# Three engines' hand-written step orders in a four-layer cross-attention kernel, placed anew

## What is computed

```python
# layer 0, per batch: channels are the 64 rows, "tokens" the 256 columns
Mn = Wn @ inorm(x) + bn ; Mm = Wm @ inorm(ctx) + bm
A  = softmax(Mn.T @ Mm)                 # 256 x 256
x  = Wo @ ((Wl @ ctx + bl) @ A.T) + bo + x
# layers 1 and 2: 16 heads of 16 features
a  = layer_norm(ctx) * gamma + beta     # over 256 features
Q, K, V = x @ Wq.T, a @ Wk.T, a @ Wv.T
x  = x + tanh(gate) * (softmax(Q K.T / 4, keys masked) V) @ Wo.T
# layer 3: one head of 256
x  = x + alpha * (softmax((x @ wq.T)(ctx @ wk.T).T / 16) (ctx @ wv.T)) @ wo.T
```

## Time and profile before

| | us |
|---|---|
| shown runs, median of 3 (lowest, highest) | 657.51 (656.33, 657.82) |
| profiled execution, its own time | 654.93 |
| its span | 653.1 |
| a round in its middle | 75.2 |
| busy: PE, DVE, ACT, POOL | 579.3, 470.0, 472.2, 118.0 |
| mean granted TensorE clock | 0.972 |

### The profile page before, as it was taken

How to read it: one execution, slowest core, us unless ns; L and a number is a source line. 1 busy time by engine, 2 the same in 40 slices (tenths; PEclk the granted TensorE clock), 3 DMA queues, 4 the chain that set the end, 5 groups by cost and what they waited for, 6 DMA issues and landing times.

```text
span 653.1 us, 25792 instructions
## 1 busy us (share of the span) xinstructions
PE 579.3 (89%) x10867; PEld 507.6 (78%) x10867; DVE 470.0 (72%) x1023; ACT 472.2 (72%) x961; POOL 118.0 (18%) x132
## 2 busy tenths in 40 slices
PE   1689988999799997999799997999989997999975
PEld 1568887978688886988689786888869886888864
DVE  4576777776696966877687766877767776968554
ACT  1589867877588866868587766878668675888571
POOL 3502060100601033100701015100511007000000
PEclk9989999999799998999989998999989999999998
DMA  6302000110020100210010100200002100001000
GB/s 164 131 3 71 2 3 8 66 35 1 3 70 3 34 2 2 71 35 2 2 44 29 34 3 2 70 19 18 2 3 70 35 2 2 3 2 35 3 2 33
DMA packets 18499, 18.32 MB, mean 28 GB/s; under 512 B 1828, under 2 KB 18340, under 8 KB 18404
## 3 DMA queue, kind: packets, MB, share of 16 engines
q1 hardware_dynamic: 18024, 16.55, 8.0%
q0 software_dynamic: 320, 0.26, 0.2%
q10 hardware_dynamic: 60, 0.01, 0.0%
HBM read 12.63 MB, written 4.19 MB: 26 GB/s over the span
## 4 chain that ended last, share of the span: by engine, by line
PE 60%; POOL 11%; DVE 11%; issue 6%; ACT 5%; DVEq 0%; POOLq 0%; ACTq 0%
PE psum L730 8%; PE psum L388 8%; PE psum L676 7%; PE psum L390 7%; PE psum L389 7%; POOL x_norm L1281 5%; PE psum L723 5%; POOL c_norm L1281 4%; PE psum L655 4%; PE psum L640 4%; DVE negmax L1054 3%; DVE shifted L1058 3%; PE psum L543 3%; PE psum L524 2%; POOL rstd L1245 2%
## 5 line engine op out<-in xcount | busy, mean ns | idle before, releaser
L1054 DVE TENSOR_REDUCE negmax<-psum 128x8 f32<-128x512 f32 x128 | 87.3, 682 | 16.0 <-PE psum L655 15.9
L1058 DVE TENSOR_TENSOR shifted<-psum,negmax 128x512 f32<-128x512 f32 x128 | 88.5, 692 | 5.4
L855 ACT ACTIVATE work<-shifted 128x512 f32<-128x512 f32 x128 | 79.0, 629 | 17.8 <-DVE shifted L1058 16.3
L869 ACT ACTIVATE work<-psum,group_mask 128x512 f32<-128x512 f32 x128 | 80.3, 694 | 14.6 <-PE psum L676 14.6
L676 PEld LDWEIGHTS psum<-const,work 64*128 64x128 f32 x1536 | 57.7, 147 | 21.4 <-issue 20.0
L676 PE MATMUL psum<-const,work 64*128 64x64 f32 x1536 | 67.3, 235 | 5.9 <-ACT work L855 4.3
L730 PEld LDWEIGHTS psum<-v,work 128*64 128x64 f32 x2048 | 63.6, 140 | 6.3 <-issue 2.4
L730 PE MATMUL psum<-v,work 128*64 128x34 f32 x2048 | 67.3, 227 | 0.0
L850 ACT ACTIVATE work<-psum,negmax 128x256 f32<-128x256 f32 x128 | 51.7, 486 | 7.9 <-DVE negmax L1050 7.7
L806 ACT ACTIVATE v<-psum 64x256 f32<-64x256 f32 x128 | 49.6, 387 | 9.1 <-PE psum L390 7.8
L1050 DVE TENSOR_REDUCE negmax<-psum 128x2 f32<-128x512 f32 x64 | 42.2, 682 | 14.5 <-PE psum L640 14.5
(11 more groups left out here) (181 smaller groups left out, 1545.6 us busy)
## 6 DMA issues: line engine op xcount, KB each, us to landing
x_raw<-in_x_dram SPq DMA_DIRECT2D x8, 512.0 KB, 4.4
c_raw<-in_ctx_dram SPq DMA_DIRECT2D x8, 512.0 KB, 5.0
out_dram<-attn SPq DMA_DIRECT2D x16, 256.0 KB, 2.7
mrow_u<-in_mask_dram SPq DMA_DIRECT2D x8, 64.0 KB, 5.4
kbd<-in_L_xattn_Wq_dram SPq DMA_DIRECT2D x2, 256.0 KB, 6.7
kbd<-in_L_xattn_Wk_dram SPq DMA_DIRECT2D x2, 256.0 KB, 7.1
kbd<-in_L_xattn_Wv_dram SPq DMA_DIRECT2D x2, 256.0 KB, 7.3
kbd<-in_L_xattn_Wo_dram SPq DMA_DIRECT2D x2, 256.0 KB, 7.7
```

The costliest lines, as they stand in the source:

```text
L855: act.activation(probs[:, exp_row(g, l, i, last), :], shifted[:, i % 2, :], ACT.Exp).then_inc(exps, 1)
L869: act.activation(probsT[:, at, :], o[:], ACT.Copy, scale=group_mask[:, 2 * i + c:2 * i + c + 1]).then_inc(free, 1)
L1054: dve.tensor_reduce(negmax[:, i % 2, :], sv, AX_X, ALU.max, negate=True).then_inc(rowmax, 1)
L1058: dve.tensor_tensor(shifted[:, i % 2, :].rearrange("t (j k) -> t j k", k=C), sv, negmax[:, i % 2, :].unsqueeze(2).broadcast_to([P, NJ, C]) ...
```

## The change

The six tables are replaced; no function, instruction or wait is changed, only where each stands. In the round: VectorE takes ST.0 after A1.0 and the rest of ST and MV.0 before O1.0; xT moves ahead of AT1.0 on TensorE and ahead of K2.0 on ScalarE; V1.1 and K3.0, K3.1 and Mm, and K1.1 and Q1.0 change places; SC.0 goes first; some exponentials of layers 0 to 2 are ordered anew among the copies; layer zero's scores S0 and products A0 are ordered anew on VectorE; H.0 moves ahead of T0.5 on ScalarE, and L.0, L.1 and PV are placed anew. The prologue's three lists are written largely anew. Since TensorE's lists change, so do the banks that the steps use.

```diff
--- before.py
+++ after.py
@@ -36,32 +36,33 @@
 
 
 PE_ORDER = """
-    V1.0 S1.0-3 V2.0 Q1.1 V3.0 S1.4-7 T1.0-1 K3.0 V1.1 A1.0-1 T1.2-3 AT1.0 K2.0 O1.0 A1.2-3 K2.1 AT1.1 Q2.0 O1.1 S2.0-3
-    xT.0-1 V2.1 V3.1 Q2.1 V0.0-1 Mn.0-1 T2.0 S2.4-7 T2.1 Mm.0-1 K3.1 A2.0-1 cT.0-1 T2.2 nT.0-1 AT2.0 T2.3 S0.0-3 A2.2-3
-    O2.0 AT2.1 K1.0 T0.0-3 S0.4-7 A0.0 S3.0 A0.1-3 T0.4-5 XN.0 O2.1 T3.0 T0.6-7 A0.4 S3.1 A0.5-7 XN.1 T3.1 Q1.0 K1.1
+    V1.0 S1.0-3 V2.0 Q1.1 V3.0 S1.4-7 T1.0-1 V1.1 K3.0 A1.0-1 T1.2-3 xT.0-1 AT1.0 K2.0 O1.0 A1.2-3 K2.1 AT1.1 Q2.0 O1.1
+    S2.0-3 V2.1 V3.1 Q2.1 V0.0-1 Mn.0-1 T2.0 S2.4-7 T2.1 K3.1 Mm.0-1 A2.0-1 cT.0-1 T2.2 nT.0-1 AT2.0 T2.3 S0.0-3 A2.2-3
+    O2.0 AT2.1 K1.0 T0.0-3 S0.4-7 A0.0-1 S3.0 A0.2-3 T0.4-5 XN.0 O2.1 T3.0 T0.6-7 A0.4 S3.1 A0.5-7 XN.1 T3.1 K1.1 Q1.0
     PV.0-1
 """
 ACT_ORDER = """
-    V1.0 X1.0 V2.0 X1.1 SC.0 Q1.1 X1.2-3 V3.0 T1.0 X1.4-5 T1.1 X1.6 K3.0 X1.7 V1.1 AT1.0 T1.2-3 H.2 K2.0 AT1.1 K2.1 Q2.0
-    xT.0 H.3 X2.0-1 xT.1 V2.1 X2.2 Q2.1 X2.3 V3.1 Mn.0-1 T2.0-1 X2.4-5 Mm.0 K3.1 Mm.1 X2.6-7 cT.0-1 T2.2 nT.0-1 AT2.0 T2.3
-    X0.0-2 AT2.1 X0.3 K1.0 T0.0-3 X0.4-5 X3.0 X0.6 T0.4 X0.7 T0.5 XN.0 T3.0 T0.6-7 H.0 X3.1 T3.1 Q1.0 XN.1 H.1 K1.1
+    SC.0 V1.0 X1.0 V2.0 Q1.1 X1.1-2 V3.0 X1.3 T1.0 X1.4-5 T1.1 X1.6 K3.0 X1.7 V1.1 AT1.0 T1.2-3 H.2 xT.0-1 K2.0 AT1.1 K2.1
+    Q2.0 H.3 X2.0 V2.1 X2.1 V3.1 Q2.1 X2.2-3 Mn.0-1 T2.0-1 X2.4 K3.1 X2.5 Mm.0 X2.6 Mm.1 X2.7 cT.0-1 T2.2 nT.0-1 AT2.0
+    T2.3 X0.0-3 AT2.1 K1.0 T0.0-3 X0.4-7 T0.4 X3.0 H.0 T0.5-7 XN.0 T3.0 X3.1 T3.1 XN.1 K1.1 Q1.0 H.1
 """
 DVE_ORDER = """
-    ST.0 S1.0-7 ST.1 A1.0-1 ST.2 AT1.0 O1.0 A1.2-3 L.2 ST.3 AT1.1 MV.0 O1.1 S2.0-1 L.3 S2.2-3 V0.0-1 Mn.0-1 S2.4-7 Mm.0-1
-    A2.0-1 cT.0-1 nT.0-1 AT2.0 S0.0-1 A2.2 S0.2 A2.3 S0.3 O2.0 AT2.1 S0.4-5 S3.0 S0.6 A0.1 S0.7 A0.3 O2.1 S3.1 L.0 X3.0
-    A0.5 X3.1 A0.7 PV.0-1 L.1
+    S1.0-7 A1.0 ST.0 A1.1 ST.1-2 AT1.0 ST.3 MV.0 O1.0 A1.2-3 L.2 AT1.1 O1.1 S2.0 L.3 S2.1-3 V0.0-1 Mn.0-1 S2.4-7 Mm.0-1
+    A2.0-1 cT.0-1 nT.0-1 AT2.0 S0.0-1 A2.2-3 S0.2-3 O2.0 AT2.1 S0.4-7 S3.0 A0.1 A0.3 O2.1 S3.1 A0.5 X3.0 L.0 X3.1 A0.7 L.1
+    PV.0-1
 """
 PE_FIRST = """
-    MT.0 GT.0 xT.0-1 MS.0 Wq1.0 cT.0-1 Wq2.0 Wk1.0 Wo3T.0 Wv2.0 W0T.0 Wv1.0 M3.0 Wk2.0 Mn.0-1 Mm.0-1 VW3.0 W0.0 S0.0-3
-    V0.0-1 VB1.0 T0.0-1 Wo2.0 T0.2-3 A0.0-1 S0.4-5 nT.0-1 S0.6-7 A0.2 Wo1.0 A0.3 T0.4-5 K1.0 VB2.0 T0.6-7 K1.1 A0.4-7 Q1.0
+    MT.0 W0T.0 GT.0 MS.0 cT.0-1 xT.0-1 W0.0 Wq1.0 Wk1.0 Wo1.0 Wq2.0 V0.0-1 Wv1.0 Wk2.0 Mn.0-1 Mm.0-1 Wo3T.0 nT.0-1 VW3.0
+    S0.0-3 M3.0 T0.0-1 S0.4-5 T0.2-3 S0.6-7 A0.0 Wv2.0 A0.1-3 T0.4-5 Wo2.0 VB1.0 T0.6-7 A0.4 K1.0 A0.5 K1.1 VB2.0 A0.6-7
+    Q1.0
 """
 ACT_FIRST = """
-    xT.0-1 Wq1.0 cT.0-1 Wk1.0 Wq2.0 Wv2.0 Wo3T.0 NM.1 NM.0 M3.0 Wk2.0 Wv1.0 TG.0 Mn.0-1 Mm.0-1 VW3.0 KB.1 X0.0-3 T0.0
-    VB1.0 T0.1-2 Wo2.0 T0.3 KB.2 nT.0-1 X0.4-7 Wo1.0 T0.4-5 H.0 T0.6-7 K1.0 OB.1 K1.1 VB2.0 Q1.0 H.1 OB.2
+    cT.0 xT.0-1 cT.1 Wq1.0 Wk1.0 NM.1 NM.0 TG.0 Wo1.0 Wq2.0 Wv1.0 Wk2.0 Mn.0-1 Mm.0-1 Wo3T.0 nT.0-1 KB.1 VW3.0 X0.0-2 M3.0
+    X0.3 T0.0-1 X0.4 T0.2-3 X0.5 Wv2.0 X0.6-7 T0.4 VB1.0 T0.5 Wo2.0 KB.2 T0.6-7 H.0 K1.0 VB2.0 OB.1 Q1.0 K1.1 H.1 OB.2
 """
 DVE_FIRST = """
-    MT.0 ST.0-2 GT.0 MS.0 ST.3 MV.0 WB.0 NB.0 cT.0 Wq1.0 cT.1 TG.0 W0T.0 Wq2.0 Wk1.0 Wv2.0 Wk2.0 M3.0 Wv1.0 Mn.0-1 Mm.0-1
-    VW3.0 ON.0 W0.0 S0.0-3 V0.0-1 Wo2.0 S0.4 A0.1 S0.5-7 nT.0-1 A0.3 Wo1.0 L.0 A0.5 A0.7 L.1
+    MT.0 WB.0 ON.0 MS.0 ST.0 W0T.0 GT.0 ST.1-2 TG.0 ST.3 MV.0 NB.0 Wq1.0 cT.0-1 W0.0 Wk1.0 Wo1.0 Wq2.0 Wv1.0 V0.0-1 Wk2.0
+    Mn.0-1 Mm.0-1 nT.0 S0.0 nT.1 S0.1-2 VW3.0 S0.3 M3.0 S0.4-7 Wv2.0 A0.1 A0.3 Wo2.0 L.0 A0.5 A0.7 L.1
 """
 AHEAD = ("H", 0), ("H", 1), ("L", 0), ("L", 1), ("Q1", 0)
 NEXT = ("xT", "cT", "nT", "Mn", "Mm", "V0", "K1", "ST", "MV")
```

## The result

| | before | after |
|---|---|---|
| median (lowest to highest), us | 656.92 (653.77 to 657.82) | 617.41 (615.99 to 619.04) |
| profiled execution: own time, span | 654.93, 653.1 | 619.04, 616.9 |
| granted TensorE clock, mean | 0.972 | 0.985 |

The ratio is 0.9407, with a 95% interval of 0.9365 to 0.945: 39 us less, for a forecast of 617.5.

A forecast was written before the change was run, and what follows sets the result against it. It took TensorE's waits and lower clock, set by VectorE's order, as the bound. 7 x 5.0 + 4.3 + 0.4 = 39.7 us off 654.93 gave 615.2, stated as 617.5 for the median; range 609 to 631.

The forecast's parts named there:

- Part 1: Statistics and moments earlier on VectorE: Mn's 3.53 us wait goes each round, and 0.66 us of lower clock.
- Part 2: Head of the iteration: of 1.14 us won at S1.4 about 0.35 is kept, since T1.0 then idles 0.85.
- Parts 3 and 4: xT ahead of AT1.0 brings V2.1 0.45 us earlier; through layer two's second half, 5.05 saved by cT.0.
- L.2 beside GpSimd: VectorE's L.2 now runs while GpSimd normalises, for which 0.25 us was added.
- Rival C: GpSimd holds VectorE's L.2 for the rest of one c_norm, 6.6 us in all: 624; chance 0.07.
- Part 5: Layer zero's products and the tail reordered: cost 0, bounded by 0 and 0.5 us a round.
- E: ScalarE's H.0 waits for A0.3 on VectorE, each round 0.5 us or more longer, some 661; chance 0.03.
- Part 6: Prologue, second half bound by ScalarE: V1.0 at 59.2, 4.3 us saved, bounds 0 and 7.
- The last round: Last iteration, without statistics and front steps: 0.4 us saved for its head.
- B: Stall goes, but VectorE and ScalarE hand part back at T1.0, T2.0, cT: 3.5 us a round, 629; chance 0.20.
- D: TensorE comes nearer its floor: 6 us a round and 5.5 in the prologue, 609; chance 0.12.
- F: MV.0 still follows AT1.0; if that came late, Mn would wait as before: 653; chance 0.03.

The follow-up runs named there:

- experiment 5: The kernel before, with 14 idle matmuls of 512 columns added on TensorE ahead of Mn's wait in each round: 649.33 us, ratio 0.9891.
- Experiment 4: The kernel before, with only the round's statistics and moments moved on VectorE and the three prologue lists replaced: 617.01 us, ratio 0.9428.
- experiment 2: The kernel before, with only VectorE's ST.0-3 and MV.0 of the round moved to their new places: 622.36 us, ratio 0.948.
- experiment 8: The changed kernel, with X1.1 ahead of Q1.1 and V3.0 behind X1.3 on ScalarE: 614.46 us, ratio 0.9381.
- experiment 7: The changed kernel, with xT.0-1 back behind S2.0-3 on TensorE and behind H.3 on ScalarE: 618.77 us, ratio 0.9454.
- experiment 9: The changed kernel, with K3.1 back behind Mm.0-1 on TensorE and between Mm.0 and Mm.1 on ScalarE: 616.29 us, ratio 0.9391.
- experiment 10: The changed kernel, with the tail of the round back in the old order on VectorE, ScalarE and TensorE: 616.42 us, ratio 0.9387.
- experiment 11: The changed kernel, with 11 and 9 idle matmuls ahead of the waits of T2.0 and T2.2 in the last round alone: 614.77 us, ratio 0.9384.
- experiment 1: The changed kernel, with only VectorE's ST.0-3 and MV.0 of the round put back to their old places: 663.68 us, ratio 1.0137.
- experiment 6: The changed kernel, with ST.3 and MV.0 put behind L.2 on VectorE, about 5 us late: 650.42 us, ratio 0.9918.

## Why the prediction was right, step by step

The sum had 35.0 in the rounds, 4.3 in the prologue, 0.4 in the last round. The profiled runs show 34.1 in the rounds, 5.2 at S1.0 (5.7 at S1.4), and -3.6 in the last round, 36.2 in all for a forecast of 39.7. Forecast and median agree within 0.1, which is luck: the profiled run came 3.8 above the 615.2 of the sum, and the median of after lies 1.6 below its profiled run, where I had put it 2.3 above.

**Part 1** was right in mechanism and place: moments at 18.65 us after S1.0, normed 1.95 ahead of Mn (I had 2.5), no wait left. It was too small in size. What the rounds say, with numbers measured one by one: 75.27 less 0.84 of clock (before's first round; experiment 5 would make it 1.03, and all that follows 0.2 lower) is 74.43, less Mn's wait of 3.53 is 70.90, less 0.44 of S1.4's wait by ST.0's leaving the head is 70.46. Experiment 4's rounds settle at 70.35 to 70.58. So statistics and moments alone are worth 4.8 a round by this sum, 4.6 as experiment 2 measured it. My walk gave them 3.53 and 0.66 and credited the rest to the steps beside them.

**Part 2**'s trade of S1.4's wait for one at T1.0 came as walked (1.04 where I had 0.85). The gain I kept, 0.35, belongs to ST.0, not to ScalarE's new order; experiment 8 reverses that order and gains 0.1 to 0.2 a round.

**Parts 3 and 4** were wrong in what they credit. The end point (cT.0) fits within 0.1 us, but putting xT and K3.1 back costs nothing (experiments 7 and 9). The step that failed is "so V2.1 comes 0.45 earlier" read as a gain. Measured at Mn it is 0.29, and the next waits for VectorE or ScalarE take all but 0.05 of it back. The walk also kept T2.1's wait of 0.49; in after that is none, and T2.0 waits 0.54 for the exponential X2.3 in its place. A walk that sums an order's steps gives its end, not what each move is worth.

**L.2 beside GpSimd,** for which I added 0.25, took 0.68 as before. Rival C is out for L.2; a smaller form of what it described exists elsewhere (below).

**Part 5** was right: 0, and experiment 10 bounds the whole tail at about 0.1 a round. H.0 (E) never waited.

**Part 6.** V1.0 on ScalarE was forecast for 59.2 and came at 58.59, X0.0 for 36.8 and came at 36.54. The timeline of ScalarE:

```profile
58.59 1.58 ACT L807 ACTIVATE v<-psum 64x256 f32<-64x256 f32 x4
```

The term was 4.3 and is about 5.2. Two of its figures were misread, and they hardly move it: between the first X0 and V1.0 ScalarE is busy for 21.5 of 22.5 us in before, not 22.3, and 22.3 less 1.7 plus 1.3 would be 21.9, not 21.7. The stretch measured 22.05, where the sum had 22.4 with its waits. Alone the prologue measured 2.8 (2.0 to 4.5 by the interval), less than 5.2. In the profiled run S1.4's longer wait (0.6) and the lower clock of the first and third round account for the difference; why the middle of ten executions shows it too is open. With the moments moved the same lists gave 3.4 by the ratios and 5.4 by the medians (experiments 2 and 4).

**The last round** was the term with the wrong sign in the profiled run: 0.4 gained for its head, 3.6 lost. I had only asked what work its head saves, and not what its own waits do to the clock. Since before's own lists gave last rounds from 56.9 to 60.56 us, the loss is in part the luck of this run; over all runs what the idle matmuls gave back is 1.5 us by the ratios and 2.6 by the medians (experiment 11).

**B** (629) fell, since the waits grew by little beyond the walk (T1.0's by 0.2, T2.0's 0.54 for T2.1's 0.49); **D** (609) fell; **F** fell with Mn's wait.

## What to carry to other kernels

When the tensor engine waits once a round for a long chain on a slow engine, find the one step that starts this chain and ask what stands before it in its engine's list: here two short steps placed 5 us later cost 4.85 us a round, and moving them with the statistics alone won 4.6. Judge every other move by undoing it alone, since time won ahead of the next cross-engine wait can be waited off there, as with xT. The worth of the others also hangs on the first: without it they cost 1.9 us a round, with it they won 0.2. Price a wait with the clock behind it, here a quarter on top, and where it can't be removed fill it with idle matmuls.

## What the runs showed of the hardware

**The clock behind a wait differs from round to round.** In before, the same wait of 3.5 us was followed by a clock of 1.00 (round of 74.43), by a short fall (75.2) and by a long one (76.39). Idle matmuls in the wait kept it at 1.00 in all seven rounds and were worth 1.0 us a round.

**VectorE and GpSimd hold each other up, depending on who starts when.** A state_lo (L.2 or L.3, two SBUF inputs) that starts within 0.05 us of one of GpSimd's four c_norm made the four take 5.35 to 5.39 instead of 4.84, in every round of experiments 1 and 6, while it took 0.68 to 0.70 itself. Started some 0.17 behind a c_norm's start it took 0.93 and c_norm none; 0.3 behind x_norm's third it took 0.80; 0.6 behind, 0.68. The Trainium skill ("SBUF — State Buffer", SBUF: two separate sides) has the two exclude each other for a whole instruction. The 0.51 to 0.55 on GpSimd is near the 0.68 of one state_lo, as that would have it. The other three cases aren't: a c_norm lasts 1.2, and no state_lo waited for the rest of one. A shorter hold would fit them: in the seven rounds of experiment 5 L.3 starts 0.14 to 0.39 behind a c_norm and takes 0.95 to 0.70, and each time it ends 1.09 to 1.10 behind that c_norm's start, the 0.68 of a free state_lo after some 0.41. That is an estimate from these rounds, and only this pair of operations shows it.
